# Spreading all eight key blocks on GpSimd, per-column scale steps, and new engine orders in a two-layer gated block

## What is computed

```python
x = x + tanh(g_xattn[0]) * performer(layernorm(x), ctx, ctx, random_features)   # 16 heads of 8, 32 features, causal
x = x + tanh(g_ffn[0])   * rwkv_channel_mix(layernorm(x), W_r, W_k, W_v, mu_r, mu_k)
x = x + tanh(g_xattn[1]) * gated_attention(ctx, layernorm(x), w_kv, w_q, w_la, w_proj, b_proj, att_weight)
x = x + tanh(g_ffn[1])   * bitnet_swiglu(layernorm(x), w_gate, w_up, w_down)    # rows rounded to 8 bits

# gated_attention, per head
attn  = softmax(q @ k.T * 8 ** -0.5)
gate  = 0.5 * mean(x @ w_la) + 0.5 * max(x @ w_la)
attn2 = softmax(gate * attn)
out   = (w * attn2 + (1 - w) * attn) @ v
```

## Time and profile before

| | us |
|---|---|
| median of 3 runs | 547.81 (545.96 to 550.05) |
| the profiled execution | 549.86 |
| its span, first to last instruction | 547.3 |

### The profile page before, as it was taken

How to read it: one execution, slowest core, us unless ns; L and a number is a source line. 1 busy time by engine, 2 the same in 40 slices (tenths; PEclk the granted TensorE clock), 3 DMA queues, 4 the chain that set the end, 5 groups by cost and what they waited for, 6 DMA issues and landing times.

```text
span 547.3 us, 17750 instructions
## 1 busy us (share of the span) xinstructions
PE 454.3 (83%) x7244; PEld 327.5 (60%) x7269; DVE 437.9 (80%) x1238; ACT 350.2 (64%) x735; POOL 341.3 (62%) x403
## 2 busy tenths in 40 slices
PE   4686989898989998889987979798979897878754
PEld 2244756574757675767665657566666665565622
DVE  5485447866998998997889989899988896969665
ACT  2333347763868877678676858776948665748444
POOL 6124535493896767696776584859666768664611
PEclk9967779997999999999899989998988897969655
DMA  7711001030101000201010011101000000000000
GB/s 197 189 50 40 22 22 40 22 82 6 42 5 50 18 25 24 69 25 34 23 42 15 4 34 49 29 12 25 22 17 1 15 15 5 7 11 11 1 10 19
DMA packets 33008, 18.22 MB, mean 33 GB/s; under 512 B 5280, under 2 KB 32800, under 8 KB 32928
## 3 DMA queue, kind: packets, MB, share of 16 engines
q1 hardware_dynamic: 32352, 17.07, 12.0%
q10 hardware_dynamic: 576, 0.02, 0.1%
HBM read 9.74 MB, written 2.10 MB: 22 GB/s over the span
## 4 chain that ended last, share of the span: by engine, by line
DVE 34%; PE 32%; POOL 13%; ACT 9%; issue 7%; DMA 3%; SPq 1%; POOLq 0%; DVEq 0%; ACTq 0%
PE MC L1595 6%; DVE WT L1014 4%; POOL kX L375 4%; PE TP L1572 4%; PE SP L1563 3%; DVE call L1068 3%; PE FP L1486 3%; PE FP L1490 3%; DVE mx L1057 3%; POOL call L405 3%; DVE emn L1077 2%; DVE ffn L1184 2%; PE MA L1517 2%; DVE ffn L1175 2%; DMA call<-in_ctx 2%
## 5 line engine op out<-in xcount | busy, mean ns | idle before, releaser
L1595 PE MATMUL MC<-Vc,ET 128*64 128x25 f32 x2048 | 77.7, 226 | 17.8 <-DVE n L1116 4.4
L1595 PEld LDWEIGHTS MC<-Vc,ET 128*64 128x64 f32 x2048 | 71.2, 148 | 33.1 <-issue 7.0
L1572 PE MATMUL TP<-ident,call 128*128 128x128 f32 x512 | 81.6, 294 | 1.9 <-POOL call L417 0.8
L405 POOL TENSOR_TENSOR call<-call,rsh 128x1024 f32<-128x1024 f32 x32 | 61.0, 1906 | 21.2 <-DVE rsh L1090 21.0
L1572 PEld LDWEIGHTS TP<-ident,call 128*128 128x128 f32 x512 | 62.4, 151 | 17.8 <-issue 9.6
L417 POOL TENSOR_TENSOR call<-call,Gs 128x1024 f32<-128x1024 f32 x32 | 61.0, 1906 | 9.4 <-DVE Gs L1106 8.1
L369 POOL TENSOR_SCALAR ft<-ft 128x512 f32<-128x512 f32 x64 | 39.8, 622 | 40.0 <-ACT ft L581 35.9
L375 POOL TENSOR_SCALAR kX<-kT,bm 128x256 f32<-128x256 f32 x64 | 58.6, 933 | 2.0 <-ACT kT L552 1.9
L1014 DVE TENSOR_TENSOR WT<-FP,mask 128x512 f32<-128x512 f32 x64 | 41.9, 677 | 4.8 <-PE FP L1503 4.5
L646 ACT ACTIVATE ET<-TP 128x512 f32<-128x512 f32 x64 | 37.3, 593 | 13.1 <-PE TP L1572 12.8
L1057 DVE TENSOR_REDUCE mx<-SP 128x16 f32<-128x1024 f32 x32 | 38.8, 1214 | 5.3 <-PE SP L1563 5.2
(11 more groups left out here) (210 smaller groups left out, 1075.5 us busy)
## 6 DMA issues: line engine op xcount, KB each, us to landing
Cd<-in_ctx SPq DMA_DIRECT2D x32, 128.0 KB, 2.9
call<-in_ctx SPq DMA_DIRECT2D x4, 512.0 KB, 8.1
xall<-in_x SPq DMA_DIRECT2D x4, 512.0 KB, 5.3
cz<-cT SPq DMA_DIRECT2D x64, 32.0 KB, 1.9
cz<-csq SPq DMA_DIRECT2D x64, 32.0 KB, 1.9
kX<-kT SPq DMA_DIRECT2D x128, 8.0 KB
out_x<-X SPq DMA_DIRECT2D x16, 128.0 KB, 2.1
ffn<-in_L_ffn_w_gate SPq DMA_DIRECT2D x1, 256.0 KB, 5.0
```

Of the source, the lines that this page charges most:

```text
L405: pool.tensor_tensor(z, E1[u].rearrange("p (h m) -> p h m", m=64), rsh[u][:, :].unsqueeze(2).to_broadcast([P, H, 64]), ALU.subtract).then_ ...
L1572: last = pe.transpose(TP[:, c:c + P], src[:, c:c + P], ident[:, :])
L1595: last = mm(MC[64 * j:64 * j + 64, c + 32 * q:c + 32 * q + 25], weights[:, q, 64 * j:64 * j + 64], Vc[g.p][:, 2 * u + j, q, 0:25], start=T ...
```

## The change

`spread` and its 128 transfers go, with the zeroing on DVE and all waits on kXd and kXz; `masked` makes all eight blocks on POOL, eight instructions a group, and each now has a second scalar operation, a multiplication by 1.0. `offset` and `quant_kh` work column by column: two `tensor_scalar` of 128 x 1 for nb, two for sg and two for kh. Semaphore counts follow (lnB, lnC and lnD reach 7 a group, kh reaches 4). Some waits that other waits already cover are left out. All six tables are new.

```diff
-            def spread(g):
-                at(sp, s("kTs"), g.k + 1)
-                at(sp, s("sc"), g.k * 4 - 4)
-                for h in (0, 1, 2, 3, 8, 9, 10, 11):
-                    sp.dma_start(kX[g.p][8 * h:8 * h + 8, h % 8, :, :].rearrange("p b m -> p (b m)"),
-                                 kT[g.p][8 * h:8 * h + 8, :]).then_inc(s(f"kXd{g.p}"), 16)
...
             def masked(g):
                 at(pool, s("kTs"), g.k + 1)
-                for h in range(4, 8):
+                for h in range(8):
                     pool.tensor_scalar(kX[g.p][:, h, :, :].rearrange("p b m -> p (b m)"), kT[g.p][:, :], bm[:, h:h + 1],
-                                       None, ALU.mult).then_inc(s("kX"), 1)
+                                       1.0, ALU.mult, ALU.mult).then_inc(s("kX"), 1)
...
             def keys(g):
-                at(act, s(f"kXd{g.p}"), g.half * 128)
                 at(act, s("pKV"), g.k + 1)
...
-            for t in kX:
-                v.memset(t[:, 0:4, :, :], 0.0).then_inc(s("kXz"), 1)
...
             def offset(n):
-                v.scalar_tensor_tensor(nb[n][:, :], mv[n][:, :, 0], -1.0, rs[n][:, :], ALU.mult, ALU.mult)\
-                    .then_inc(s(f"ln{n}"), 1)
+                for u in range(2):
+                    v.tensor_scalar(nb[n][:, u:u + 1], mv[n][:, u, 0:1], rs[n][:, u:u + 1], -1.0, ALU.mult, ALU.mult)\
+                        .then_inc(s(f"ln{n}"), 1)
...
             def quant_kh(g):
-                at(v, s("hx1"), g.k * 5)
                 at(v, s("am"), g.k * 3 + 2)
-                v.tensor_scalar(sg[:, :], amc[:, :], wgu[:, 0:1], 0.5, ALU.mult, ALU.mult).then_inc(s("kh"), 1)
-                v.scalar_tensor_tensor(kh[:, :], amc[:, :], wcc[:, 0:1], amc[:, :], ALU.mult, ALU.mult)\
-                    .then_inc(s("kh"), 1)
+                for u in range(2):
+                    v.tensor_scalar(sg[:, u:u + 1], amc[:, u:u + 1], wgu[:, 0:1], 0.5, ALU.mult, ALU.mult).then_inc(s("kh"), 1)
+                for u in range(2):
+                    v.tensor_scalar(kh[:, u:u + 1], amc[:, u:u + 1], wcc[:, 0:1], amc[:, u:u + 1], ALU.mult, ALU.mult)\
+                        .then_inc(s("kh"), 1)
...
             def scores(g, u):
-                if u == 0:
-                    at(pe, s(f"kXd{g.p}"), g.half * 128 + 128)
                 if u == 0:
                     at(pe, s("QT"), g.k + 1)
-                    at(pe, s("kX"), g.k * 4 + 4)
...
-            strips(G[3]); strips(G[4]); load(G[4]); strips(G[5]); load(G[5]); strips(G[6]); load(G[6])
-            rows(2); spread(G[2]); strips(G[7]); load(G[7]); spread(G[3]); strips(G[8]); store(G[0])
+            strips(G[0]); strips(G[1]); load(G[2]); strips(G[2]); strips(G[3]); load(G[3]); strips(G[4])
+            load(G[4]); strips(G[5]); load(G[5]); rows(2); strips(G[6]); load(G[6]); store(G[0])
```

More of the change, by code:

```diff
@@ L448, in _ @@
[L448 to L452, removed]
@@ new lines, in _ @@
+            pe.wait_ge(s("fe"), 20); values(G[3]); scores(G[2], 0)
+            pe.wait_ge(s("n2"), 4); ffn_dn(G[0], 0)
+            pe.wait_ge(s("kTs"), 4); weights0(G[4], 0); rows_BT(G[3]); ffn_down(G[0], 1)
+            pe.wait_ge(s("WT"), 17); rows_T(G[5]); ffn_dn(G[0], 1); project_T(G[1])
+            pe.wait_ge(s("ls"), 5); scores(G[2], 1); ffn0_in(G[3])
+            pe.wait_ge(s("oT"), 2); turn1(G[2], 0); turn1(G[2], 1)
+            pe.wait_ge(s("out"), 2); project(G[1]); weights0(G[4], 1)
@@ new lines, in _ @@
+            pe.wait_ge(s("oT"), 5); ffn_down(G[3], 1)
+            pe.wait_ge(s("out"), 7); project(G[4])
+            pe.wait_ge(s("ls"), 11); scores(G[5], 1)
+            pe.wait_ge(s("Vc"), 14); features(G[8], 0); turn1(G[5], 0)
+            pe.wait_ge(s("X3"), 5); ffn_dn(G[3], 1); turn1(G[5], 1)
+            pe.wait_ge(s("fe"), 34); features(G[8], 1); turn1(G[5], 2)
+            pe.wait_ge(s("F"), 22); turn1(G[5], 3)
+            pe.wait_ge(s("out"), 8); outA(G[5], 0); ffn0_in(G[6])
+            pe.wait_ge(s("n1"), 11); outA(G[5], 1); ffn_in(G[4]); ffn0_out(G[6]); ffn_gu(G[4], 0)
@@ new lines, in _ @@
+            pe.wait_ge(s("out"), 13); project(G[7]); ffn_down(G[6], 1)
+            pe.wait_ge(s("WT"), 44); values(G[9]); rows_BT(G[9])
+            pe.wait_ge(s("X3"), 8); ffn_dn(G[6], 1)
+            pe.wait_ge(s("ls"), 17); scores(G[8], 1)
+            pe.wait_ge(s("Vc"), 20); features(G[11], 0); turn1(G[8], 0); turn1(G[8], 1)
+            pe.wait_ge(s("fe"), 46); features(G[11], 1)
+            pe.wait_ge(s("out"), 14); outA(G[8], 0); turn1(G[8], 2); turn1(G[8], 3); ffn0_in(G[9])
+            pe.wait_ge(s("fe"), 48); rows_T(G[12])
@@ new lines, in _ @@
+            pe.wait_ge(s("n2"), 23); outB(G[11], 1)
+            pe.wait_ge(s("WT"), 58); weights0(G[14], 1); queries(G[12]); project_T(G[11]); ffn_dn(G[10], 0)
+            scores(G[12], 0)
+            pe.wait_ge(s("oT"), 12); ffn_down(G[10], 1)
+            pe.wait_ge(s("out"), 21); project(G[11])
+            pe.wait_ge(s("WT"), 60); values(G[13]); rows_BT(G[13])
+            pe.wait_ge(s("X3"), 12); ffn_dn(G[10], 1)
+            pe.wait_ge(s("ls"), 25); scores(G[12], 1)
+            pe.wait_ge(s("Vc"), 28); features(G[15], 0); turn1(G[12], 0); turn1(G[12], 1)
@@ new lines, in _ @@
+            pe.wait_ge(s("hg"), 24); rows_CT(G[13])
+            pe.wait_ge(s("n2"), 25); outB(G[12], 1); queries(G[13])
+            pe.wait_ge(s("WT"), 62); weights0(G[15], 1); project_T(G[12]); ffn_dn(G[11], 0); scores(G[13], 0)
+            pe.wait_ge(s("out"), 23); project(G[12]); ffn_down(G[11], 1)
+            pe.wait_ge(s("WT"), 64); values(G[14])
+            pe.wait_ge(s("X3"), 13); ffn_dn(G[11], 1)
+            pe.wait_ge(s("ls"), 27); scores(G[13], 1); rows_BT(G[14]); turn1(G[13], 0); turn1(G[13], 1)
```

1159 lines of the change are left out of this document (520 added, 639 removed).

## The result

The changed kernel takes **577.8 us** (571.4 to 582.4, 4 runs) against 547.7 us for the kernel before: a ratio of **1.051** (95% interval 1.040 to 1.061). It is 5% slower; forecast were 533 us and 2.7% less. The profiled execution spans 569.4 us, at a mean granted TensorE clock of 0.876 (before: 547.3 us at 0.894).

A forecast was written before the change was run, and what follows sets the result against it. Dependencies between engines in a given order were taken to bound the kernel, no engine being full. 549.9 - 3 - 2.5 - 4 - 1 - 5 = 534.4 us; against the median 532.3, rounded up to 533, range 512 to 560.

The forecast's parts named there:

- The orders: New orders on all engines: a tenth of DVE's middle-stretch idle gained, 5 us; bounds 10 us lost to 27 gained.
- the 63 that the prediction named: Sign: DVE idle between 60 us and the last features over 63 us means shorter distance turned into waits; about 48 expected.
- The releasers named: If shorter distance became waits, PE's and POOL's rows for rs_D, shifted and ffn_dn would name them.
- The spread: Key spread on POOL: 128 two-operation steps at 406 ns, 52.0 us for 58.6, gaining 2.5 us.
- The rival that the column operand is slow: Spread on POOL: the column operand keeps a block at 933 ns, so 558 us, up to 575; 18%.
- The transfers: The 128 key transfers land under other work: removal worth nothing, plus 3 us from SP's queue.
- The wait for xall: DVE's wait for the third quarter of x, queued behind strips, should go; gain nothing to 3.6 us, 3 taken.
- The scale steps: nb, kh and sg on DVE by single columns aren't held by POOL; 4 us gained, lower bound nothing.
- the 0.25 named: Sign on DVE: no nb, sg or kh row over some 0.25 us; otherwise holding did not make them long.
- The drain: Behind the last features PE has 117 calls for 129; about 1.2 us gained, 1 taken.

The follow-up runs named there:

- E1: Kernel before, own orders, with all new operations: eight key blocks spread by GpSimd in two-operation form, no key transfers, single-column offset and quant_kh; 546.4 us, ratio 0.992.
- E8: Changed kernel with six extra 512-column matmuls, result unused, ahead of TensorE's wait for n1 in seven groups; 559.5 us, ratio 1.015.
- E10: Changed kernel with gated_G's product Gs computed by GpSimd, not VectorE; 558.1 us, ratio 1.017.
- E5: Kernel before, own orders and two-column steps, with all eight key blocks spread by GpSimd in two-operation form and no key transfers; 546.6 us, ratio 0.999.
- E12: E1 with the spread back to one operation, no second scalar; 615.4 us, ratio 1.122.
- E15: Kernel before with one edit: the second scalar operation on GpSimd's four spread blocks, transfers kept; 533.2 us, ratio 0.973.
- E16: Kernel before with single columns, filled TensorE waits and two-operation spread on four blocks (519.5 us), plus third input-row load ahead of group 6's strips; 521.2 us.
- E6: Kernel before, own orders and spread, with only offset and quant_kh done column by column; 544.1 us, ratio 0.982.
- E2: Changed kernel with the old two-column forms of offset (nb) and quant_kh (sg, kh); 584.8 us, ratio 1.068.
- E3: Changed kernel with quant_clip (amc) also done column by column; 576.8 us, ratio 1.046.
- E4: Changed kernel with VectorE's first moved ahead of the quant steps and gated_G at 29 places; 580.9 us, ratio 1.065.
- E7: Changed kernel with the second half of features put directly ahead of TensorE's wait for n1 in seven groups; 601.5 us, ratio 1.100.

## Why the prediction was wrong

- **The orders (forecast: 5 us gained, at worst 10 lost).** This step of the sum failed, and by itself it decides: the new orders lost 31 us (577.8 against E1's 546.4). Its bound was taken from DVE's idle time alone, 0.7 us a group. That part came nearly as bounded: 63.9 us of idle in the middle stretch for 53.5, just over the 63 that the prediction named as the sign of a shorter distance turned into waits. The releasers named were wrong: DVE waits 1.6 us for rs_D and 6.0 for `ffn_dn` (1.9 and 8.6 before), and `shifted` isn't in its list; what grew are waits for other steps of PE and ACT. Adding up VectorE's list of waits by the engine that ended them, over the whole span, gives for E1 PE 41.4, POOL 25.2, ACT 16.4 us, and for the changed kernel PE 69.3, POOL 13.8, ACT 23.5. TensorE's own waits moved the other way, to ACT (35.5 for 22.0) and POOL (19.7 for 13.4), away from DVE (28.4 for 37.4). The longest rows of VectorE's list in the changed kernel (total us, times, longest); in E1 the same five take 4.6, 2.6, 1.4, 1.7 and 5.0 us:

```profile
DVE ffn L1155 <- ACT ffn L661: 20.1, 24, 3.6
DVE ext L1007 <- PE MA L1496: 11.7, 8, 3.8
DVE vr L1036 <- PE MA L1518: 11.4, 8, 2.2
DVE rs L1105 <- PE MC L1571: 10.3, 11, 3.1
DVE WT L1001 <- PE FP L1484: 9.4, 15, 1.8
```

- **What the bound left out.** It held PE's and DVE's work constant. Both grew: PE by 18.8 us against E1, since the gaps let its clock fall and a fall lasted up to 13.6 us; and DVE's small steps by 9.0 us in all, since the new orders put Gs, amc and ve_C beside POOL's long rows (15.4 us more, of which ve_B, ve_D and rsh gave back 6.4). By the fit the clock is 14 us of the loss, (150 - 96) x 0.26 with the medians of the time at half clock; E8 and E10 each took back 18 to 20 us. The granted clock stands in the earlier trace rows, and the prediction made no term of it.
- **The spread (2.5 us gained).** The mechanism was right, the price off: two operations are cheap, but 481 to 485 ns and not 406. (The row of 406 ns writes bf16 and has no column operand, the new step writes f32 and has one; which of the two costs the 80 ns was not tried.) So 128 blocks cost 59.3 us for 58.6 and the term is zero, as E5 shows. The rival that the column operand is slow fell with E12. What I had not seen: the second operation on the old four blocks, with the transfers left alone, gains 14 us (E15), and moving the other four blocks from the transfers onto POOL spends just that (E5). POOL's time was worth 14 / (58.6 - 29.6) = 0.48 us a us, near the 22 / 58.6 = 0.38 of the chain.
- **The transfers (nothing, plus 3 us for xall).** Nothing is right: in E5 they are gone, POOL's spread costs as much as before, and the time is the same. In E15 they spare POOL four blocks, and that kernel is 13 us under E5. The wait for xall went as foretold and gave nothing (E16): the wait was on the chain, but another took its place.
- **The scale steps (4 us).** Right: 5 us (medians) to 10 us (ratio) in the old orders (E6), and 4 by the ratios of E1 and E5; 7 in the new ones (E2), not clear of noise. Nb stays within 115 to 216 ns; kh, at 264, is a little over the 0.25 named. But other steps took over part of the holds: in E1 ve_B, ve_D and rsh take 21.8 us for 16.2 before. The Trainium skill (SBUF — State Buffer, Who interferes with whom) says that a `tensor_scalar` may be shut out when it runs in a two-port mode, and any DVE instruction with two SBUF inputs by a GpSimd one that reads. The trace agrees: amc with two columns up to 1524 ns, in E3 one column at 138 ns in the mean; Gs with two inputs up to 1.8 us. Which mode an instruction ran in, the trace doesn't show.
- **The drain (1 us).** 125.4 us behind the last `features` for 124.3: nothing. Against E1, where 118.2 us follow the last `features` in the old order, the new orders lose 7 us here, so part of their loss lies in the drain.

What stays open: at equal clock the changed kernel is 535 us, E10 528 and E1 512. The 16 us between E10 and E1 are neither the held Gs nor, by the fit, the clock. The longer waits of VectorE for PE and ACT, and of TensorE for ACT and POOL, are where they should lie, and the shorter distance between stages would explain them; no run lengthened that distance alone, so this is argued, not shown. Nor was it tried which engine's order matters: the orders leave out waits that the others make needless, so they can't be mixed.

## What to carry to other kernels

A new order must be costed with the clock in it: list TensorE's gaps, look at what the granted clock does behind each, and count the work there at the lower level. Taking one wait away is not enough if the next one opens (E4, E7); work that nobody needs, put into the wait, gained more (E8). And price each half of a double edit by itself: here the cheap form of an instruction was worth 14 us, and its second half, moving more work onto that engine, gave all of it back.

## What was not expected of the hardware

- In the middle stretch of the changed kernel the clock fell at single gaps of 1.2 to 2.7 us on TensorE, and at two places behind several of at most 0.65 us. How long it stayed down differed: 13.6 us behind the gap of 2.73 us at 321 us, but 3.5 us (321.75 to 325.25) in the kernel before, behind a gap of 2.67 us that ended at 322.17. The size of the gap alone doesn't tell it, and what does was not found.
- GpSimd's `tensor_scalar` on 128x256 f32 takes 925 ns with one operation and 481 ns with two (E12, E1). The Trainium skill (GPSIMD Engine Reference, Elementwise — side-by-side cycle accounting) holds a loop of up to two operations to be bound by its port, by which both would take the same; these rows differ, and they decide.
- A hold on VectorE by GpSimd is not removed by making one step immune to it: part of it goes to the next step that can be held (from nb to ve_B, ve_D and rsh in E1, 5.6 us of it; from amc to Gs in E3, 2.4 us).
